# Convolution stage in one block, pipelined over the batches

## The reference, cut to what matters

```python
# block L0: a linear non-local block, then batch norm over batches and positions, plus the input
f  = einsum('bni,bim->bnm', theta_x, phi_x) / n       # theta, phi, g: 64 channels from 128
y  = einsum('bnm,bmi->bni', f, g_x)
wy = einsum('ci,bihw->bchw', w_w, y) + w_b
x  = (wy - mean) * rsqrt(var + 1e-5) * gamma + beta + x
# block L1, on g = group_norm(x, 32 groups)
freq  = (2x2 mean pool of g, to 16 x 16) . dct, lowest 4 x 4
f     = sigmoid(relu(freq @ w_f1 + b_f1) @ w_f2 + b_f2)
route = softmax(relu(f @ w_r1 + b_r1) @ w_r2 + b_r2)  # 8 weights for each batch
dyn_k = einsum('be,eoihw->boihw', route, experts)     # a 3x3 kernel 128 -> 128 per batch
x     = x + conv3x3(g, dyn_k)
# then attention, a token feed-forward, a second attention, a mixture of experts
```

## Time and profile before

| | us |
|---|---|
| median of 3 runs | 2735.08 |
| lowest and highest | 2731.08, 2741.87 |
| span of the profiled execution | 2741.1 |
| from the span's start to the end of the last copy to T (the convolution stage and the constants) | 190.68 |
| busy in the span: PE, DVE, ACT, POOL | 2453.0, 1883.0, 1459.0, 1308.2 |

### The profile page before, as it was taken

How to read it: one execution, slowest core, us unless ns; L and a number is a source line. 1 busy time by engine, 2 the same in 40 slices (tenths; PEclk the granted TensorE clock), 3 DMA queues, 4 the chain that set the end, 5 groups by cost and what they waited for, 6 DMA issues and landing times. The chain is left out here.

```text
span 2741.1 us, 52000 instructions
## 1 busy us (share of the span) xinstructions
PE 2453.0 (89%) x16743; PEld 1695.4 (62%) x16743; DVE 1883.0 (69%) x3715; ACT 1459.0 (53%) x2524; POOL 1308.2 (48%) x884
## 2 busy tenths in 40 slices
PE   5499996855899999999999999999999999999857
PEld 3366663544566666666666666666666666666755
DVE  2767763677476776867768677687776776867626
ACT  1114552332366657666576665766657666566323
POOL 0213782000246647457375573755737547366435
PEclk8699997967999999999999999999999999999779
DMA  3004210011431121111211202112021120212233
GB/s 113 1 6 93 62 33 9 1 46 58 106 90 43 36 52 35 43 45 26 52 35 43 56 15 52 35 43 56 15 52 35 43 56 15 52 35 47 76 109 97
DMA packets 85075, 131.56 MB, mean 48 GB/s; under 512 B 16224, under 2 KB 60768, under 8 KB 84624
## 3 DMA queue, kind: packets, MB, share of 16 engines
q1 hardware_dynamic: 81328, 123.16, 17.9%
q0 software_dynamic: 3024, 7.43, 0.9%
q10 hardware_dynamic: 656, 0.09, 0.0%
HBM read 63.49 MB, written 20.79 MB: 31 GB/s over the span
## 5 line engine op out<-in xcount | busy, mean ns | idle before, releaser
L2498 ACT ACTIVATE a_PT<-PS 128x512 f32<-128x512 f32 (+1 forms) x1111 | 613.6, 585 | 353.3 <-PE PS L2363 227.8
L2216 POOL TENSOR_TENSOR a_KT<-a_PT 128x512 f32<-128x512 f32 (+2 forms) x179 | 418.5, 2354 | 473.9 <-ACT a_PT L2498 464.8
L2216 POOL TENSOR_TENSOR a_KT<-a_KT,a_PT 128x2048 f32<-128x2048 f32 (+3 forms) x128 | 391.8, 3061 | 8.8
L2567 DVE TENSOR_REDUCE a_NM<-PS 128x2 fp32r<-128x512 f32 x460 | 296.8, 686 | 127.2 <-PE PS L2311 123.6
L2357 PE MATMUL PS<-a_QH,a_KSW 128*128 128x256 f32 (+2 forms) x848 | 287.5, 358 | 13.2 <-DVE a_NM L2567 12.5
L2357 PE MATMUL PS<-a_QH,a_K 128*128 128x512 f32 (+3 forms) x768 | 295.4, 395 | 0.0
L2581 DVE TENSOR_REDUCE a_MX<-PS 128x1 f32<-128x512 f32 (+3 forms) x432 | 265.7, 664 | 34.3 <-PE PS L2322 19.8
L2358 PE MATMUL PS<-a_QL,a_K1B 76*128 76x512 f32 (+3 forms) x768 | 259.6, 348 | 0.0
L2322 PE MATMUL PS<-a_K,a_QH 128*128 128x512 f32 (+3 forms) x768 | 254.7, 407 | 1.6
L2554 DVE TENSOR_TENSOR a_KSW<-PS,a_KSW 64x512 fp32r<-64x512 f32 x170 | 117.2, 690 | 124.2 <-ACT a_KSW L2457 121.0
L2308 PE MATMUL PS<-a_KSW,a_QH 128*128 128x512 f32 x460 | 198.6, 480 | 3.5 <-DVE a_QL L2551 3.5
(11 more groups left out here) (435 smaller groups left out, 5368.9 us busy)
## 6 DMA issues: line engine op xcount, KB each, us to landing
a_KWB<-a_KSW SPq DMA_DIRECT2D x68, 256.0 KB, 3.3
a_K1B<-a_K SPq DMA_DIRECT2D x32, 512.0 KB, 5.3
a_XC<-latents SPq DMA_DIRECT2D x17, 512.0 KB, 3.9
a_CKS<-latents SPq DMA_DIRECT2D x17, 512.0 KB, 4.6
a_CF<-latents SPq DMA_DIRECT2D x17, 448.0 KB, 4.1
slots<-in_empty_slots SPq DMA_DIRECT2D x1, 5160.0 KB, 19.7
f_XB<-slots SPq DMA_DIRECT2D x8, 645.0 KB, 4.1
c_EX<-in_experts SPq DMA_DIRECT2D x1, 4608.0 KB, 17.6
```

Source lines behind the costliest of these rows:

```text
L2216: nc.gpsimd.tensor_tensor(total, one_in, other_in, ALU.add).then_inc(s["added"], 1)
L2498: nc.scalar.activation(PT[:, to:to + width], turning(key)[:, 0:width], ACT.Exp).then_inc(s["taken"], 1)
L2567: ins = nc.vector.tensor_reduce(out, bank.rearrange("p (a n) -> p a n", a=2), AX.X, ALU.max, negate=True)
```

## The change

The constants' block is gone, and their loads go into the stage. The two blocks of the stage become one.

- Loads: SP issues PG, the four batches of x, `ident`, the experts, and then the other constants. ACT issues the other small weights (15 loads).
- PE starts with 9 products on a zeroed bf16 tile. ACT takes one Sqrt of a constant after its loads.
- The projections are written out by hand in a skewed order over the batches, with a buffer for each batch (PT has two).
- Batch norm: one `scalar_tensor_tensor` for each batch, X = WY * scale + X. The shift is left out of X. It is added to the statistics, taken off the mean, and added back in `add_conv`.
- Each batch is pooled right behind its write to XP. POOL starts its four subtractions only when all four batches are pooled.
- The hold of the clock is split, 36 products behind the group statistics and 30 ahead of the convolution.
- The kernel is mixed in two chunks of columns, 4 taps and 5 taps. KDL is made by DVE in the middle of the next chunk's mixing, no longer by POOL. The turning of a batch goes behind the first chunk of the next one.

In the diff below the calls that make up the order of PE and of DVE in the projections are joined on fewer lines, and some arguments are cut to `...`.

```diff
+CHUNKS = ((0, 4), (4, TAPS))
@@ one block now; SP and ACT
+                sp.dma_start(PG[:, :], d["pg_w"]).then_inc(ld_first, 16)
                 for b in range(B):
                     sp.dma_start(X[:, b * N:(b + 1) * N], d["x"][:, b * N:(b + 1) * N]).then_inc(ld_x[b], 16)
+                sp.dma_start(ident[:, :], d["ident"]).then_inc(ld_c, 16)
                 sp.dma_start(EX[:, :, :].rearrange("p e n -> p (e n)"), d["experts"]).then_inc(ld_e, 16)
+                for dst, src in ((maskf[:, :, :], d["masks"]), (lohi[:, :], d["lohi"]), (tri[:, :], d["tri"]), (below[:, :], d["below"])):
+                    sp.dma_start(dst, src).then_inc(ld_c, 16)
...
+                for dst, src in ((PGb, d["pg_b"].broadcast_to([128, 2 * CI])), (wwT, d["w_wT"]), (thw, d["theta_w"]),
+                                 (thb, d["theta_b"]), (vec, d["vec"])):
+                    act.dma_start(dst[:, :], src).then_inc(ld_first, 16)
@@ PE
+                pe.wait_ge(warm_set, 1)
+                for _ in range(9):
+                    nc.tensor.matmul(P[7][:, :], warm[:, 0:128], warm[:, :], start=True, stop=True)
+                project(0), project(1), gram(0), project(2), middle(0), gram(1), weight(0), project(3), middle(1), output(0),
+                gram(2), weight(1), middle(2), output(1), gram(3), weight(2), middle(3), output(2), weight(3), output(3)
...
@@ PE: behind the product with blk4, ahead of the transposes of pp
+                hold_clock(nc, P[7], ident, 36)
@@ PE: convolution
-                hold_clock(nc, P[7], ident, 60)
+                hold_clock(nc, P[7], ident, 30)
+                for k, (b, n) in enumerate(jobs):        # jobs: (batch, chunk)
+                    pe.wait_ge(image_low, b + 1)
+                    pe.wait_ge(kernel_low, k + 1)
...
+                    if b and n == 0:
+                        turn(b - 1)
+                turn(B - 1)
@@ DVE: projections
+                add_bias(0), add_bias(1), keep_gram(0), add_bias(2), scale_middle(0), keep_gram(1), bias_of(0), add_bias(3),
+                scale_middle(1), moments(0), keep_gram(2), bias_of(1), scale_middle(2), moments(1), keep_gram(3), bias_of(2),
+                scale_middle(3), moments(2), bias_of(3), link(moments(3))
@@ DVE: batch norm
-                for k in range(0, B * N, N):
-                    nc.vector.tensor_scalar(WY[:, k:k + N], WY[:, k:k + N], sc[:, 0:1], sc[:, 3:4],
-                                            ALU.mult, ALU.add).then_inc(bn_done, 1)
-                for i, k in enumerate(range(0, B * N, N)):
-                    dve.wait_ge(bn_done, i + 1)
-                    nc.vector.tensor_tensor(X[:, k:k + N], X[:, k:k + N], WY[:, k:k + N], ALU.add).then_inc(bn_done, 1)
+                for b in range(B):
+                    k = b * N
+                    nc.vector.scalar_tensor_tensor(out=X[:, k:k + N], in0=WY[:, k:k + N], scalar=sc[:, 0:1], in1=X[:, k:k + N],
+                                                   op0=ALU.mult, op1=ALU.add).then_inc(bn_done, 1)
@@ DVE: image and pooling, per batch
+                for b in range(B):
+                    nc.vector.tensor_scalar(XP[:, b, 1:1 + HW, 1:1 + HW], ...).then_inc(padded, 1)
+                    dve.wait_ge(padded, b + 1)
                     link(nc.vector.tensor_tensor(pr[:, b, :, :], ...))
                     nc.vector.tensor_tensor(pp[:, b, :]...).then_inc(pooled, 1)
@@ POOL
+                pool.wait_ge(pooled, B)
                 for b in range(B):
                     pool.wait_ge(image_high, b + 1)
                     nc.gpsimd.tensor_tensor(flat(XPL, b), flat(XP, b), flat(XPH, b).bitcast(F32), ALU.subtract)
@@ DVE: mixing
+                def low_kernel(k):
+                    b, n = jobs[k]
+                    dve.wait_ge(kernel_high, k + 1)
+                    nc.vector.tensor_tensor(part(KDL, b, n), part(KD, b, n), part(KDH, b, n).bitcast(F32), ALU.subtract)
+                for k, (b, n) in enumerate(jobs):
+                    if b >= 2 and n == 0:
+                        dve.wait_ge(kernel_low, len(CHUNKS) * (b - 1))
...
+                        if e == 2 and k:
+                            low_kernel(k - 1)
+                    ins.then_inc(mixed, 1)
+                    if b and n == len(CHUNKS) - 1:
+                        add_conv(b - 1)                   # scalar_tensor_tensor: PSUM + shift + X
+                low_kernel(len(jobs) - 1)
+                add_conv(B - 1)
@@ program: the block of constants is removed
```

More of the change, by code:

```diff
@@ L166, in _ @@
+                for k, (b, n) in enumerate(jobs):
+                    act.wait_ge(mixed, k + 1)
+                    if b >= 2:
+                        act.wait_ge(conv_ready, 2 * (b - 1))
+                    nc.scalar.activation(part(KDH, b, n), part(KD, b, n), ACT.Copy).then_inc(kernel_high, 1)
+                    if b >= 2 and n == 1:
+                        keep_turned(b - 2)
+                keep_turned(B - 2)
+                keep_turned(B - 1)
             @block.gpsimd
             def _(pool):
+                nc.gpsimd.memset(warm[:, :], 0.0).then_inc(warm_set, 1)
@@ L304, in _, with turn @@
                 last.then_inc(lg_ready, 1)
-                hold_clock(nc, P[7], ident, 60)
-                for b in range(B):
+                def turn(b):
+                    for u in range(2 * b, 2 * b + 2):
+                        pe.wait_ge(conv_added, u + 1)
+                        if u >= 2:
+                            pe.wait_ge(t_copied, u - 1)
+                        for t in range(4):
+                            k = (4 * u + t) * 128
+                            last = nc.tensor.transpose(P[4 + u % 2][:, t * 128:(t + 1) * 128], X[:, k:k + 128], ident[:, :])
+                        last.then_inc(t_ready, 1)
@@ L314, in _ @@
                             dy, dx = divmod(tap, 3)
[L315 removed]
+                            for term, (kernel, image) in enumerate(((KDH, XPH), (KDH, XPL), (KDL, XPH))):
                                 last = nc.tensor.matmul(P[2 * (b % 2) + h][:, :], kernel[:, b % 2, tap * C:(tap + 1) * C],
                                                         image[:, b, 16 * h + dy:16 * h + dy + 16, dx:dx + HW],
[L318 removed]
@@ L372, in add_conv @@
-            def add_conv(nc, dve, b):
-                for h in range(2):
-                    k = b * N + h * HALF
-                    dve.wait_ge(conv_ready, 2 * b + h + 1)
-                    nc.vector.tensor_tensor(X[:, k:k + HALF], X[:, k:k + HALF], P[2 * (b % 2) + h][:, :], ALU.add)\
-                        .then_inc(conv_added, 1)
+                                                        start=(tap == 0 and term == 0), stop=(tap == TAPS - 1 and term == 2))
+                        if n == len(CHUNKS) - 1:
+                            last.then_inc(conv_ready, 1)
@@ new lines, in moments @@
+                def moments(b):
+                    for h in range(2):
+                        k = b * N + h * HALF
+                        dve.wait_ge(wy_copied, 2 * b + h + 1)
+                        ins = nc.vector.bn_stats(st[:, 2 * b + h, :], WY[:, k:k + HALF])
+                    return ins
+                dve.wait_ge(ld_first, 16 * 6)
+                add_bias(0)
+                add_bias(1)
+                keep_gram(0)
+                add_bias(2)
+                scale_middle(0)
@@ new lines, in _ @@
+                keep_gram(1)
+                bias_of(0)
+                add_bias(3)
+                scale_middle(1)
+                moments(0)
+                keep_gram(2)
+                bias_of(1)
+                scale_middle(2)
+                moments(1)
+                keep_gram(3)
+                bias_of(2)
+                scale_middle(3)
+                moments(2)
+                bias_of(3)
+                link(moments(3))
+                link(nc.vector.bn_aggr(mv[:, :], st[:, :, :].rearrange("p a s -> p (a s)")))
```

351 lines of the change are left out of this document (175 added, 176 removed).

## The result

| | before | after |
|---|---|---|
| median of the runs, us | 2735.08 (2731.08 to 2741.87) | 2716.13 (2713.81 to 2723.13) |
| profiled execution: time, span | span 2741.1 | 2715.15, 2713.3 |
| stage: last copy to T ends | 190.68 | 147.48 |
| rest of the span | 2550.4 | 2565.8 |

The ratio is 0.9936, 95% interval 0.9918 to 0.9954. The forecast was 2690 (2679 to 2710). The stage did what was forecast (145.35 was named, 147.48 measured), but the rest, whose code for each operation is unchanged, took 15.4 us longer.

A forecast was written before the change was run, and what follows sets the result against it. Five stretches of the stage, each bound differently: 7.0 + 31.0 + 14.65 + 22.0 + 70.7 = 145.35 against 190.68, 45.3 less, passed on in full: 2695.8 profiled, 2690 beside the median; range 2679 to 2710.

The forecast's parts named there:

- (a): Start of the stage: PE's first projection begins at 7.0 us instead of 15.7, bounds 6 and 10.
- (b): Projections of the four batches in skewed order: 31.0 us instead of 49.7, bounds 27.4 and 47.6.
- Rivals 1 and 5: Projections: clock stays at half, 2706, chance 0.11; or an in-order DVE wait keeps batches following each other, 2708, 0.04.
- (c): Batch norm and group statistics, two passes becoming one: 14.65 us instead of 17.3 (14.4 to 15.6).
- (d): Image, pooling and router, up to the mixing weights: 22.0 us instead of 33.0 (20 to 26).
- (e): Convolution with two-chunk mixing, DVE becoming the bound: 70.7 us instead of 75.0, bounds 69 and 76.
- Rival 4: Convolution: new waits lose PE its clock for good, so slower than before, 2756; chance 0.03.
- rival 2: DVE and POOL obstruct each other more, chunks cost more: (d) 26, (e) 76, (a) 10; 2702, chance 0.11.

The follow-up runs named there:

- Run 8: Changed kernel with the two constant casts on ACT, small loads awaited where first read, and the repeated row made as a maximum: 2711.18 us (0.9904).
- runs 8 and 10: Run 8 and, on the changed kernel with the two constant casts on ACT, KDL's subtractions on POOL again in two chunks: 2695.69 us (0.9862).

## Why the prediction was wrong, step by step

- **(a) start, 7.0: measured 10.79, mis-sized.** x was there; `vec`, the last of the five small loads, went out at 3.17, where I had 2.7, and took 7.6 us from issue to landing, where I took 4.4 from the earlier trace rows. My upper bound of 10 was short too. Run 8 shows the cause.
- **(b) projections, 31.0: measured 28.6** (10.79 to 39.37). The order worked as walked, and the clock, 1.00 over the stretch, was better than the 7 us at half that I added. Rivals 1 and 5 fall.
- **(c) batch norm, 14.65: 14.4** (39.37 to 53.79). The new operation took 1.28, I had 1.22.
- **(d) image to weights, 22.0: 22.5.** The pooling took 0.69 and 0.43 a batch, unheld. The repeated row waited for POOL: 1.09, not 0.42. So the half of the rule that no row showed (the copy with one input) holds here. The Trainium skill, page SBUF — State Buffer, section "SBUF: two separate sides", names both kinds, the two-port modes and two SBUF inputs against a GpSimd operation that reads SBUF; runs 8 and 10 agree on both. The step named the softmax's subtraction as what waits for POOL, and it came 2 us behind it.
- **(e) convolution, 70.7: 71.2.** DVE had no gap through the mixing, 15.5 us a batch, and PE waited for DVE's remainder four times, 5.9 in all and 2.2 the longest, and kept a clock of 0.99 over the stretch. Rival 4 falls, and rival 2 has only its part (a).
- **The step that failed:** "What the convolution stage gains is therefore passed on in full, as long as the later stages see the same state." The stage gave 43.2, 2.1 less than forecast. The later stages run the same operations, but at another place in DVE's code. This cost 25.2 us, more than half of the gain. With the loop one instruction further on the kernel takes 2691.15, 1 us from the forecast, and this nearness is partly luck. It is one execution, and its last stage, whose code for each operation is that of before, took 171.3 us against 178.8. Without that the profiled execution would lie near the 2695.8 that the sum gave; its span is 2688.9. The last sentence of the prediction had this as its own test (the rest changes by more than 5), but no rival gave it a price.
- Of the rest's 15.4 us, 25.2 are the batch ends; some 2 came back in the stages ahead of them, and the last stage gave back 7.5 (178.8 to 171.4). The last stage took 171.0 to 180.5 us in the thirteen profiled executions (171.0 to 177.9 at the bad starts, 171.3 to 180.5 at the others), so this part doesn't follow the place of the attention's loop. 4.4 of the 7.5 is one wait of DVE ahead of `f_A`, which the profile puts down to a transfer (11.47 in before, 7.11 in after). What moves it stays open. The word "issue" misleads here: before has a wait of 3.44 for "issue" at another `f_A`, but it ends as PE's product ahead of it ends, and after has it too (3.43, put down to PE).

## What to carry to other kernels

A change that lengthens an engine's code moves every loop behind it. When a stage shows its gain and the whole doesn't, line up the starts of the same operations in both traces. If the difference steps at loop ends with idle time put to "issue" and the instruction queue has new packets at those times, add one or a few empty instructions ahead of the loop and measure again. Small loads that share one semaphore release the first consumer only when the last has landed; wait for each where it is first read.

## What was unexpected of the hardware

- One instruction of 0.1 us, off every path, is worth 24 us of span (2713.3 and 2688.9): two stalls of about 3.4 us at each of three batch ends, one of 2.7 at the fourth, and the lower clock of PE behind them. Bad starts were 1424 and 1425, and again 1552 and 1553; 1426, 1437, 1441 and 1485 were good, and 1423 had one stall of 2.8 us at the final exit.
- The edge between two pieces costs only where it falls behind the inner loop's last branch and not behind the outer's. Why the inner loop's own returns cost nothing when it runs over the same edge in every pass (1426) stays open.
- Handing work from DVE to POOL made DVE slower: a POOL operation of 1.6 or 1.7 us held DVE for 1.0 to 1.2 (1.45 less 0.48, 6.63 less 5.47), and what it took over was 0.7 to 0.8.
- In the start, five loads of 0.2 to 64 KB issued beside x landed 2.6, 4.6, 5.7, 6.9 and 7.6 us after issue, in their order.
